# A second attention whose SP queue issues the next loads between the rows of maxima and the second shares, with the rows in one transfer

## The chip, the cores and the metric

The kernel runs on one core of a Trainium2 chip. Its engines are TensorE (PE in the profile; PEld is its weight load), VectorE (DVE), ScalarE (ACT), GpSimd (POOL) and SyncE (SP). SP computes nothing here: it waits on semaphores and issues DMA transfers, in the order in which they are written. The metric is the device time of one execution in microseconds (us), as the median of several runs.

## The reference, cut to what matters

Two transformer layers over 4 sequences of 1024 tokens with 256 columns. Each layer is attention and then a feed-forward part, with a layer norm behind each. The second layer's attention, which the change touches, has 8 heads of 32 columns:

```python
scores = jnp.einsum('bhqd,bhkd->bhqk', q, k) * scale
causal = jnp.tril(jnp.ones((T, T), dtype=bool))
scores = jnp.where(causal[None, None], scores, -jnp.inf)
...
attn = jax.nn.softmax(scores, axis=-1)
out = jnp.einsum('bhqk,bkhd->bqhd', attn, v).reshape(B, T, C)
return out @ w_out
```

The product with w_out, a residual sum, a layer norm and the routing of tokens to 16 experts follow on the same tokens, and then the experts themselves.

## The kernel before

The function phase_layer1 computes the second attention in 16 groups: 4 sequences (batches) times 4 pairs of heads. A group takes 12 rounds on PE, numbered i = 0 to 11. A round multiplies one tile of keys with a block of 512 queries for both heads (L2822, into PS), ACT takes the exponential (L2919), POOL masks the diagonal tiles (L2874), and some rounds later PE multiplies with the values (L2801, into PO).

**Maxima run ahead.** A softmax needs each query's maximum before its exponentials. PE therefore computes plain score products (L2774, into one of two tiles PM) for a group one or two ahead, twelve tiles for each group, and DVE reduces each tile (take, L2958). PE may write a tile of PM only when DVE has taken what stood in it. In the rounds 0 to 5 of group g these products belong to group g + 1, and from round 6 on to group g + 2: at round 6 PE waits for the queries and keys of group g + 2 (the semaphore q_in). In round 7 PE transposes the finished maxima of group g + 1 (L2785), ACT copies them to mrows (L2903), and SP sends them as two extra rows under the queries of that group (rows, L2711). They are needed at round 0 of group g + 1.

**Loads.** Queries, keys and values have 4 buffers. load(g) issues three transfers of queries, three of keys (256 KB each, L1558) and one of values (512 KB, L1569): 2 MB. SP issues load(g + 3) in group g.

**Sums and shares.** When a half (512 queries) of a group is done, ACT copies it out (L2911) and SP sends the row totals (L1785) and the unnormalised sums (L1790) to their places. DVE inverts the totals (L1917), SP stores them to DRAM (L1797, store_shares), waits for that, and reads them back spread over 32 partitions for each head (L1810, load_shares, 128 KB). Half 0 of group g - 1 is fetched at the start of SP's pass for group g, half 1 of group g - 1 behind the rows of group g + 1. When all four groups of a batch have their shares, DVE multiplies sums with shares (L1939, "weigh"): half 0 in round 7 and half 1 in round 11 of the first group of the next batch, that is of the groups 4, 8 and 12. These instructions stand in DVE's one queue between the reductions of L2958. PE then projects with w_out (L1849).

**Order.** There is no scheduler. Each engine's program is a Python loop, and an engine runs its instructions in the order in which that loop wrote them; SP's loop is the one in the function under block.sync.

The lines on which round 6 and the weighing wait are these:

```python
if t == 0 and ahead <= left:
    pe.wait_ge(q_in[(g + ahead) % BUFS], ((g + ahead) // BUFS + 1) * Q_TURNS)
...
dve.wait_ge(self.sums_in[i], self.SUM_DMAS * HG1 * (b + 1))
dve.wait_ge(self.shares_in[i], 16 * HG1 * (b + 1))
```

Of the kernel before, what the change touches and what calls it, by code (L numbers as in the profile page):

```python
# [6 lines left out]
F32 = mybir.dt.float32  # L7
# [11 lines left out]
TPB = SEQ // P  # L19
# [22 lines left out]
HALVES1 = 2  # L42
# [514 lines left out]
def phase_attention0(nc, d, keep, weights, stacks, shared):  # L557
# [25 lines left out]
    MROWS = R0 * PAIRS0 * HALVES1 * TPH  # L583
    ROW_DMAS = 16 * R0 * PAIRS0
    ONES_DMAS = 16 * BUFS * R0
# [31 lines left out]
    def head_of(g, s):  # L617


        return s % G0 if g == GROUPS - 1 and s // G0 > WIDE_FROM // G0 else ORDER[s % G0]  # L620
# [44 lines left out]
    with ExitStack() as ctx:  # L665
# [104 lines left out]
        def _(pool):  # L770
# [27 lines left out]
            for u in range(TURNS):  # L798
                cut_maxima(u)
                if u in FETCHES:  # L800

                    pool.wait_ge(rows_in, (u + 1) * ROW_DMAS)
                    weights.fetch(pool, d, FETCHES[u])
# [8 lines left out]
                if 0 <= first < ZERO_DMAS:  # L812
# [3 lines left out]
                    else:  # L816
                        pool.wait_ge(zero_out, 16 * first)
                    pool.wait_ge(rows_in, (u + 1) * ROW_DMAS)
                    for n in range(first, first + BLANKS):
# [14 lines left out]
        def _(pe):  # L834
# [44 lines left out]
            def score(g, s):  # L879
# [4 lines left out]
                if s % (UNITS // HALVES) == 0:  # L884
                    pe.wait_ge(rows_in, (HALVES * g + half + 1) * ROW_DMAS)
                p, r = head_of(g, s) // R0, head_of(g, s) % R0
# [58 lines left out]
        def _(act):  # L945
# [6 lines left out]
            def copy_rows(u):  # L952
                mine = slice(u % HALVES * MROWS, (u % HALVES + 1) * MROWS)
                act.wait_ge(m_turned, u + 1)
                if u >= HALVES:
                    act.wait_ge(rows_in, (u + 1 - HALVES) * ROW_DMAS)
                act.activation(mrows[mine], PT[mine], ACT.Copy).then_inc(m_copied, 1)
# [76 lines left out]
G1 = 2  # L1034
# [516 lines left out]
def load_keys1(sp, d, g, q, k, arrived):  # L1551


    hg, tok = g % HG1, slice(g // HG1 * SEQ, (g // HG1 + 1) * SEQ)
    for stack, side, first_blk in ((q, 0, 0), (k, 1, 2)):
        for s, pair in enumerate(PAIRS1):
            rows = d["qk1"][pair[side] * 4 + first_blk + hg // 2, (hg % 2) * 64:(hg % 2) * 64 + 64, tok]
            sp.dma_start(stack[s * D1:(s + 1) * D1].bitcast(F32), rows.rearrange("(j p) n -> p j n", p=D1)).then_inc(arrived, 16)  # L1558
# [8 lines left out]
def load_values1(sp, d, g, v, arrived):  # L1567
    src = values1(d, g // HG1)[g % HG1]
    sp.dma_start(v[:].rearrange("p t j c -> p (t j c)"), src.rearrange("p i c -> p (i c)")).then_inc(arrived, 16)  # L1569
# [1022 lines left out]
def phase_layer1(nc, d, keep, weights, tokens, shared):  # L2592


    K = len(PAIRS1) * D1
    KM = K + HALVES1
    BUFS = HG1
# [13 lines left out]
    GAP = SBANKS  # L2611
    TURN_PLACE = (TURN + 1) * G1
    LAPS = UNITS + GAP
    ROW_DMAS = 16 * HALVES1
    Q_TURNS = K1_TURNS
    LATE_TOTALS = (10, 6)
    assert STEPS % MTILES == 0 and LAPS % SBANKS == 0 and UNITS % RING == 0 and ROUNDS % PAIRED == 0
# [39 lines left out]
    with ExitStack() as ctx:  # L2657
# [3 lines left out]
        qst = [shared.q1] + [a.sb(f"qst{i}", [P, G1, SEQ], F32R) for i in range(1, BUFS)]  # L2661
# [7 lines left out]
        mrows = a.sb("mrows", [HALVES1 * G1 * TPB, P])  # L2669
# [12 lines left out]
        m_step, m_cut, m_turned, m_copied, rows_in = (  # L2682
            a.sem(n) for n in ("m_step", "m_cut", "m_turned", "m_copied", "rows_in"))
        scores, exped, masked, pv_done, out_copied = (
            a.sem(n) for n in ("scores", "exped", "masked", "pv_done", "out_copied"))
        route = Routing(nc, ctx, const, weights, tokens, shared, PM, max_taken, entry)
# [13 lines left out]
        @block.sync  # L2700
        def _(sp):
            def load(g):
                hg = g % BUFS
                load_keys1(sp, d, g, qst[hg], kst[hg], q_in[hg])
                load_values1(sp, d, g, vst[hg], v_in[hg])

            def rows(g):

                sp.wait_ge(m_copied, g + 1)
                for i in range(HALVES1):  # L2710
                    sp.dma_start(qst[g % BUFS][K + i:K + i + 1].bitcast(F32), mrows[i * G1 * TPB:(i + 1) * G1 * TPB, :])\  # L2711
                      .then_inc(rows_in, 16)

            def sums(g, half):
                sp.wait_ge(out_copied, g * HPS + half + 2)
                route.send_sums(sp, outT, g, half)

            sp.wait_ge(shared.ffn_stored, shared.FFN_DMAS)
            load(1)
            rows(0)  # L2720
            load(2)
            route.load_weights(sp, d)
            for g in range(GROUPS):
                if g > 0:
                    sums(g - 1, 1)
                    route.load_shares(sp, d, g - 1, 0)
                    route.store_shares(sp, d, g - 1, 1)
                sums(g, 0)
                if g + 1 < GROUPS:
                    rows(g + 1)  # L2730
                if g > 0:
                    route.load_shares(sp, d, g - 1, 1)
                if g + BUFS - 1 < GROUPS:
                    if g > 0:

                        sp.wait_ge(pv_done, g * ROUNDS + RING // G1)
                    load(g + BUFS - 1)
                if g == GROUPS - 3:
                    route.wait_sums_free(sp, BATCH - 2)
                    weights.load_up(sp, d, bass.ds(0, 1), 0)  # L2740
                if g == GROUPS - 2:
                    route.wait_shares_free(sp, BATCH - 2)
                    weights.load_down(sp, d, bass.ds(0, 1), 0)
                route.store_shares(sp, d, g, 0)
            route.load_shares(sp, d, GROUPS - 1, 0)
            sums(GROUPS - 1, 1)
            route.store_shares(sp, d, GROUPS - 1, 1)
            route.load_shares(sp, d, GROUPS - 1, 1)
            for n in range((BATCH - 1) * HPS, BLOCKS):
                sp.wait_ge(route.x3_done, (n + 1) * TPK)  # L2750
                tokens.store(sp, d, n, tokens.last_x3_out)
            route.wait_sums_free(sp, BATCH - 1)
            route.wait_shares_free(sp, BATCH - 1)
            weights.load_up(sp, d, bass.ds(1, 1), 1)
            weights.load_down(sp, d, bass.ds(1, 1), 1)
            sp.wait_ge(route.scattered, 16 * TOP_K * TILES)
            experts_sp(sp)

        @block.tensor
        def _(pe):  # L2760
# [45 lines left out]
            def slot(g, i):  # L2806
# [3 lines left out]
                if i == 0:  # L2810
                    pe.wait_ge(rows_in, (g + 1) * ROW_DMAS)
                ahead, t = 1 + (AHEAD + i) // STEPS, (AHEAD + i) % STEPS
# [183 lines left out]
def program(nc, d):  # L2996
    d["shares0"] = nc.dram_tensor("shares0", [H0, TOKENS], F32).ap()
    d["sums1"] = nc.dram_tensor("sums1", [SUM_ROWS, DIM], F32).ap()
    d["shares1"] = nc.dram_tensor("shares1", [H1, TOKENS], F32).ap()
    d["halves0"] = nc.dram_tensor("halves0", [HALVES1 * QK_BLK, P, TOKENS], F32).ap()  # L3000
    with ExitStack() as ctx:
        keep = {"const": ctx.enter_context(nc.sbuf_tensor("const", [P, C_COLS], F32))}
        shared = Shared(nc, ctx)
        with ExitStack() as layer0:
            weights = Layer0Weights(nc, layer0)
            with ExitStack() as attention:
                stacks = Stacks0(nc, attention, shared)
                phase_qkv0(nc, d, keep, stacks, shared)
                phase_attention0(nc, d, keep, weights, stacks, shared)
            phase_ffn0(nc, d, keep, weights, shared)  # L3010
        with ExitStack() as layer1:
            weights = ExpertWeights(nc, layer1, shared)
            tokens = Routed(nc, layer1, shared)
            phase_layer1(nc, d, keep, weights, tokens, shared)
# [54 lines left out]
```

## Time and profile before

| | |
|---|---|
| median of 3 runs | 1913.09 us (1911.92 to 1913.39) |
| profiled execution | 1909.37 us, its span 1907.4 us |
| second attention in the span | about 1143 to 1536 us |
| PE busy share of the span | 94% |
| DVE, ACT, POOL busy share | 75%, 59%, 28% |

Times in rows are counted from the span's start. What an engine waited for stands in brackets behind the row of the instruction that waited. "SPq" rows are instructions that issue transfers; their duration is that of the issue, not of the transfer. A granted TensorE clock of 1.00 is 2.4 GHz, 0.50 is 1.2 GHz.

### The profile page before, as it was taken

The numbers are of one execution on the slowest core, as the hardware profiler recorded it, in microseconds if no ns is written. First come the engines' busy times: TensorE is split into PE (matmuls) and PEld (weight loads), VectorE is DVE, ScalarE is ACT, GpSimd is POOL, SyncE is SP. The second block draws the span as 40 slices with busy tenths as digits, with TensorE's granted clock in tenths as the row PEclk, the third lists the DMA queues.
The fourth block names the chain that finished last, engine by engine and source line by source line (L and its number), as shares of the span: only waits on it lengthen the run. The fifth ranks groups of instructions, "written<-read, shape, count | busy, mean of one in ns | idle before, by whom it ended". The sixth has DMA issues, their size and how long they took to land. (4 is left out here: it accounts for less than half of the span.)

```text
span 1907.4 us, 34604 instructions
## 1 busy us (share of the span) xinstructions
PE 1795.9 (94%) x12690; PEld 1170.9 (61%) x12690; DVE 1429.7 (75%) x2814; ACT 1117.3 (59%) x2212; POOL 528.6 (28%) x686
## 2 busy tenths in 40 slices
PE   8989999999999999799999989999999987999994
PEld 4545444444444444388888865555555566999994
DVE  7879999999999999367677655466666554766665
ACT  4645888888888888622333214446463632655555
POOL 5760000233000001032223212212525243444444
PEclk9986999999999999899999988999999998999997
DMA  4883744565434502023444255546666334655555
GB/s 170 280 260 53 124 79 96 131 144 122 86 57 73 83 28 85 20 76 111 153 143 147 89 188 120 137 100 156 153 154 156 97 107 147 150 144 144 145 115 196
DMA packets 146600, 239.18 MB, mean 125 GB/s; under 512 B 25830, under 2 KB 81159, under 8 KB 146449
## 3 DMA queue, kind: packets, MB, share of 16 engines
q1 hardware_dynamic: 113312, 171.48, 36.8%
q0 software_dynamic: 17024, 34.25, 7.0%
q10 hardware_dynamic: 16112, 31.46, 4.5%
q8 instruction: 92, 1.51, 0.3%
q14 instruction: 60, 0.48, 0.1%
HBM read 137.49 MB, written 96.60 MB: 123 GB/s over the span
## 5 line engine op out<-in xcount | busy, mean ns | idle before, releaser
L994 DVE TENSOR_REDUCE b_mx<-b_PM 128x1 f32<-128x512 f32 x1024 | 621.0, 679 | 17.9 <-PE b_PM L848 17.5
L970 ACT ACTIVATE b_probs<-b_PS 128x512 f32<-128x512 f32 x1000 | 523.9, 606 | 69.1 <-PE b_PS L902 53.8
L848 PE MATMUL b_PM<-b_kst,b_qst 48*128 48x512 f32 x888 | 280.9, 430 | 0.0
L2919 ACT ACTIVATE d_probs<-d_PS 128x512 f32<-128x512 f32 (+3 forms) x384 | 166.5, 496 | 183.2 <-PE d_PS L2822 182.5
L902 PE MATMUL b_PS<-b_qst,b_kst 50*128 50x512 f32 x744 | 256.9, 436 | 2.1 <-issue 0.2
L2958 DVE TENSOR_REDUCE d_mx<-d_PM 128x2 f32<-128x1024 f32 (+1 forms) x192 | 179.9, 950 | 101.5 <-PE d_PM L2774 59.3
L902 PEld LDWEIGHTS b_PS<-b_qst,b_kst 50*128 50x128 f32 x744 | 120.4, 184 | 163.4 <-ACT b_probs L970 147.4
L2874 POOL TENSOR_SCALAR_AFFINE_SELECT d_probs<-d_probs 128x128 f32<-128x128 f32 x256 | 74.6, 305 | 268.1 <-ACT d_probs L2919 263.4
L790 POOL CAST b_mhalves<-b_maxima 128x16 fp32r<-128x16 f32 x32 | 6.3, 197 | 505.3 <-DVE b_maxima L1003 505.3
L848 PEld LDWEIGHTS b_PM<-b_kst,b_qst 48*128 48x128 f32 x888 | 142.0, 184 | 5.4
L874 PE MATMUL b_PO<-b_probs,x_v 128*32 128x384 f32 (+2 forms) x2048 | 145.2, 390 | 0.0
L874 PE MATMUL b_PO<-b_probs,b_vst 128*32 128x384 f32 (+3 forms) x1960 | 143.0, 397 | 1.0 <-ACT b_probs L970 0.9
L1257 POOL TENSOR_TENSOR c_hT<-c_hidden,c_hT 128x512 fp32r<-128x512 f32 x48 | 64.8, 1350 | 218.1 <-DVE c_hT L1504 218.1
L2562 DVE TENSOR_TENSOR f_h_low<-f_h,f_h_high 128x512 fp32r<-128x512 f32 x96 | 66.5, 692 | 72.8 <-ACT f_h_high L2352 72.8
L2822 PE MATMUL d_PS<-d_qst,d_kst 98*128 98x512 f32 (+3 forms) x288 | 106.3, 386 | 8.6 <-ACT d_probs L2919 4.1
L2385 POOL DMA_INDIRECT sums<-f_y,f_to x44 | 88.8, 2019 | 90.2 <-ACT f_y L2333 72.2
L848 PE MATMUL b_PM<-x_k,x_q 48*128 48x512 f32 x291 | 108.0, 508 | 3.0 <-DVEq L986 2.7
L2774 PE MATMUL d_PM<-d_kst,d_qst 96*128 96x512 f32 (+3 forms) x288 | 102.0, 372 | 3.0 <-DVE d_mx L2958 3.0
L902 PE MATMUL b_PS<-x_q,x_k 50*128 50x512 f32 x256 | 91.5, 448 | 0.6
L2822 PEld LDWEIGHTS d_PS<-d_qst,d_kst 98*128 98x128 f32 x288 | 53.9, 191 | 49.9 <-issue 32.5
L1276 PE MATMUL c_PG<-c_x1T,u_w_gate 128*128 128x512 f32 x288 | 76.7, 402 | 5.5 <-DVE c_hidden L1502 4.1
L2333 ACT ACTIVATE f_y<-f_y,f_coef 128x256 f32<-128x256 f32 x44 | 22.4, 510 | 95.2 <-DVE f_y L2540 95.2
(318 smaller groups left out, 3753.9 us busy)
## 6 DMA issues: line engine op xcount, KB each, us to landing
halves<-a_parts SPq DMA_DIRECT2D x7, 2048.0 KB, 8.7
qk<-c_halves ACTq DMA_DIRECT2D x7, 2048.0 KB
w_w<-L_ffn_fc1T SPq DMA_DIRECT2D x12, 1024.0 KB, 5.0
w_w<-L_ffn_fc2T SPq DMA_DIRECT2D x12, 1024.0 KB, 6.3
b_qst<-halves SPq DMA_DIRECT2D x72, 128.0 KB, 4.4
b_kst<-halves SPq DMA_DIRECT2D x72, 128.0 KB, 7.6
d_qst<-qk SPq DMA_DIRECT2D x36, 256.0 KB, 5.2
d_kst<-qk SPq DMA_DIRECT2D x36, 256.0 KB, 7.4
```

The costliest lines, as they stand in the source:

```text
L848: mm = pe.matmul(PM[n % MBANKS][:], qst[buf][at, p, first:first + P], kst[buf][at, p, kh * BLK:(kh + 1) * BLK], start=True, stop=True)
L874: mm = pe.matmul(PO[j * VS0:(j + 1) * VS0, cols], vst[g % BUFS][:, kt, j, :], probs[:, (R * G0 + i) % RING, cols], start=(kt == 0 and firs ...
L902: pe.matmul(score_bank(g, s)[:], kst[g % BUFS][at, p, kt * P:(kt + 1) * P], qst[g % BUFS][at, p, half * BLK:(half + 1) * BLK], start=True, ...
L970: act.activation(probs[:, s % RING], score_bank(g, s)[:], ACT.Exp).then_inc(exped, 1)
L994: dve.tensor_reduce(mx[:, half, (r * PAIRS0 + p) * TPH + t, kh:kh + 1], PM[n % MBANKS][:], AX.X, ALU.max)\
L1276: mm = pe.matmul(out, lhs(left, c), rhs(right, c), start=(k == 0 and c == 0), stop=(k == len(PAIRS1) - 1 and c == chunks - 1))
L2385: pool.indirect_dma_start(out=d["sums1"], out_offset=bass.IndirectOffsetOnAxis(ap=index.bitcast(U32), axis=0), in_=src, in_offset=None, bo ...
L2774: mm = pe.matmul(PM[n % MTILES][:, j, 0:w], qst[g % BUFS][0:K, j, qt * P:(qt + 1) * P], kst[g % BUFS][0:K, j, kh * BLK:kh * BLK + w], star ...
L2822: pe.matmul(PS[bank(s)][:, 0:w], kst[g % BUFS][0:KM, j, kt * P:(kt + 1) * P], qst[g % BUFS][0:KM, j, q0:q0 + w], start=True, stop=True).th ...
L2874: pool.affine_select(out=near, in_=near, pattern=[[1, P]], compare_op=ALU.is_ge, fill=0.0, base=0, channel_multiplier=-1)\
L2919: act.activation(probs[:, s % RING, 0:w], PS[bank(s)][:, 0:w], ACT.Exp).then_inc(exped, 1)
L2958: dve.tensor_reduce(mx[:, :, qt, kh], PM[n][:, :, 0:keys(qt, kh)], AX.X, ALU.max).then_inc(max_taken[n], 1)
```

## The change

In each group's pass of SP's loop, the load of group g + 3, with its wait on pv_done, now stands directly behind the rows of maxima, and load_shares for half 1 of group g - 1 behind the load; before it was the other way round. The two row transfers (one for the high halves, one for the low halves) become one transfer with two destination partitions, and the count that the readers wait for is halved to match.

```diff
-    ROW_DMAS = 16 * HALVES1
+    ROW_DMAS = 16
...
                 sp.wait_ge(m_copied, g + 1)
-                for i in range(HALVES1):
-                    sp.dma_start(qst[g % BUFS][K + i:K + i + 1].bitcast(F32), mrows[i * G1 * TPB:(i + 1) * G1 * TPB, :])\
-                      .then_inc(rows_in, 16)
+                sp.dma_start(qst[g % BUFS][K:KM].rearrange("i j n -> i (j n)").bitcast(F32), mrows[:]).then_inc(rows_in, 16)
...
                 if g + 1 < GROUPS:
                     rows(g + 1)
+                if g + BUFS - 1 < GROUPS:
+                    if g > 0:
+
+                        sp.wait_ge(pv_done, g * ROUNDS + RING // G1)
+                    load(g + BUFS - 1)
                 if g > 0:
                     route.load_shares(sp, d, g - 1, 1)
-                if g + BUFS - 1 < GROUPS:
-                    if g > 0:
-
-                        sp.wait_ge(pv_done, g * ROUNDS + RING // G1)
-                    load(g + BUFS - 1)
```

SP's queue in the pass for group 4, before. x_q1_60 and its like are the query and key buffers of the first group of four, d_qst1 to d_qst3 those of the others; w_w2 holds the shares and w_w1 the sums:

```order
L1790 DMA w_w1<-d_outT 32x512 x2
L2711 DMA d_qst1<-d_mrows 1x16x128 x2
L1810 DMA w_w2<-shares1 64x1x512
L1558 DMA d_qst3<-qk1 32x2x1024 x3
L1558 DMA d_kst3<-qk1 32x2x1024 x3
L1569 DMA d_vst3<-v1 128x1024
L1797 DMA shares1<-e_totals 2x64x8
```

The same place now:

```order
L2710 DMA d_qst1<-d_mrows 2x16x128
L1558 DMA d_qst3<-qk1 32x2x1024 x3
L1558 DMA d_kst3<-qk1 32x2x1024 x3
L1569 DMA d_vst3<-v1 128x1024
L1810 DMA w_w2<-shares1 64x1x512
L1797 DMA shares1<-e_totals 2x64x8
```

The seven transfers of a load have moved ahead of the one that fetches shares, and two row transfers are one. The passes for the groups 1 to 12 change in this way; those for 13 to 15 have no load, and in the pass for group 0 there are no shares to fetch.

DVE's queue in rounds 6 to 12 of the same group 4, where the shares are used (L2958 is a reduction of maxima, L1939 the weighing, L1952 the residual sum of the projected block, L1946 statistics for the norm):

```order
L2958 TENSOR_REDUCE d_mx<-d_PM 128x2 x2
L1917 RECIPROCAL e_totals<-e_totals 128x8
L1952 TENSOR_TENSOR e_x<-e_x,d_PM 128x1024
L2958 TENSOR_REDUCE d_mx<-d_PM 128x2
L1939 TENSOR_TENSOR w_w<-w_w 128x512
L1946 BN_STATS e_stats<-e_x 128x6 x2
L2958 TENSOR_REDUCE d_mx<-d_PM 128x2
L1939 TENSOR_TENSOR w_w<-w_w 128x512
L1946 BN_STATS e_stats<-e_x 128x6 x2
L2958 TENSOR_REDUCE d_mx<-d_PM 128x2 x2
```

Nothing moved here: the changed kernel has the same rows with line numbers that are lower by two for the lines of phase_layer1.

## Rows read from the trace of the kernel before

**Rows 1.** The page: the span, and the chain that ended last by engine.
```profile
span 1907.4 us, 34604 instructions
...
PE 28%; DVE 4%; DMA 4%; ACT 2%; issue 2%; SPq 1%; POOL 1%; POOLq 0%; DVEq 0%; ACTq 0%
```

**Rows 2.** Waits, 1140 to 1535 us: engine, line, releaser; total us, times, longest.
```profile
PE d_PS L2822 <- DMA d_kst<-qk: 6.4, 3, 2.8
```

**Rows 3.** Timeline of PE, round 6 of groups 2, 3, 8, 12: start, duration, instruction, wait.
```profile
1204.15 0.50 PE L2822 MATMUL d_PS<-d_qst,d_kst 98*128 98x512 f32 x1 [1.74 <-DMA x_k<-qk]
...
1227.26 0.50 PE L2822 MATMUL d_PS<-d_qst,d_kst 98*128 98x512 f32 x1 [2.76 <-DMA d_kst<-qk]
...
1349.18 0.50 PE L2822 MATMUL d_PS<-x_q,x_k 98*128 98x512 f32 x1 [1.66 <-DMA d_kst<-qk]
...
1450.45 0.50 PE L2822 MATMUL d_PS<-x_q,x_k 98*128 98x512 f32 x1 [1.97 <-DMA d_kst<-qk]
```

**Rows 4.** Timeline of SP, pass of group 4.
```profile
1255.15 1.22 SPq L2711 DMA_DIRECT2D d_qst<-d_mrows  x2
1256.41 0.57 SPq L1810 DMA_DIRECT2D w_w<-shares  x1
1257.03 1.37 SPq L1558 DMA_DIRECT2D d_qst<-qk  x3
...
1259.85 0.43 SPq L1569 DMA_DIRECT2D d_vst<-v  x1
1261.00 0.56 SPq L1797 DMA_DIRECT2D shares<-e_totals  x1
```

**Rows 5.** Timelines of SP and of DVE: a fetch of shares with quiet queues.
```profile
1250.37 0.56 SPq L1810 DMA_DIRECT2D w_w<-shares  x1
...
1255.17 0.69 DVE L1939 TENSOR_TENSOR w_w<-w_w 128x512 f32<-128x512 f32 x1 [2.22 <-DMA w_w<-shares]
```

**Rows 6.** Windows: stretch, us; PE, PEld, DVE, ACT, POOL busy; PEclk, DMA share, GB/s.
```profile
1254.00:1255.00 1.00, 1.00 (x6) 0.37 (x3) 0.00 (x0) 0.00 (x0) 0.00 (x0) 1.00 0.17 25
1258.00:1268.00 10.00, 10.00 (x57) 6.91 (x54) 6.38 (x10) 3.10 (x8) 2.38 (x8) 1.00 0.99 215
```

**Rows 7.** Timeline of SP, pass of group 2: a store behind a load, and its waiter.
```profile
1217.71 0.56 SPq L1797 DMA_DIRECT2D shares<-e_totals  x1
...
1229.13 0.56 SPq L1810 DMA_DIRECT2D w_w<-shares  x1
```

**Rows 8.** The chain in order of time: the same store with quiet queues.
```profile
1533.64 4.67 DMA shares<-e_totals
```

**Rows 9.** DMA issues of groups 4, 8, 12: the values; the last number is us to landing.
```profile
d_vst<-v SPq DMA_DIRECT2D x1, 512.0 KB, 10.4
...
d_vst<-v SPq DMA_DIRECT2D x1, 512.0 KB, 11.6
...
d_vst<-v SPq DMA_DIRECT2D x1, 512.0 KB, 10.9
```

**Rows 10.** Timeline of DVE, round 11 of group 4: half 1 is weighed.
```profile
1264.63 0.68 DVE L1939 TENSOR_TENSOR w_w<-w_w 128x512 f32<-128x512 f32 x1
```

**Rows 11.** Timeline of PE, group 5, round 2: the product, then the projection.
```profile
1268.04 0.40 PE L2774 MATMUL d_PM<-d_kst,d_qst 96*128 96x512 f32 x1
...
1269.62 3.69 PE L1849 MATMUL d_PM<-e_wout,w_w 128*128 128x256 f32 x16 [0.83 <-DVE d_mx L2958]
```

**Rows 12.** Windows with the granted clock (PEclk), columns as in Rows 6.
```profile
1204.00:1208.00 4.00, 3.61 (x21) 2.02 (x21) 0.43 (x1) 2.66 (x6) 0.00 (x0) 1.00 0.21 65
1228.00:1234.00 6.00, 6.00 (x19) 2.45 (x18) 1.32 (x3) 2.76 (x6) 0.00 (x0) 0.50 0.16 41
1351.00:1354.00 3.00, 3.00 (x11) 1.13 (x11) 0.76 (x2) 1.38 (x4) 1.02 (x2) 0.51 0.31 110
1453.00:1456.00 3.00, 3.00 (x8) 0.64 (x8) 0.76 (x2) 0.65 (x3) 0.29 (x1) 0.50 0.23 76
1545.00:1548.00 3.00, 2.95 (x7) 2.41 (x8) 2.97 (x3) 0.00 (x0) 2.39 (x3) 0.52 0.21 66
```

**Rows 13.** Timeline of PE behind the last group: what came before the last window.
```profile
1545.05 5.41 PE L1849 MATMUL d_PM<-e_wout,w_w 128*128 128x256 f32 x16 [2.00 <-DVE w_w L1939]
```

More of the change, by code:

```diff
@@ L2730, in _ @@
                     rows(g + 1)
-                if g > 0:
-                    route.load_shares(sp, d, g - 1, 1)
                 if g + BUFS - 1 < GROUPS:
@@ L2737, in _ @@
                     load(g + BUFS - 1)
+                if g > 0:
+                    route.load_shares(sp, d, g - 1, 1)
                 if g == GROUPS - 3:
```

## The prediction

> **What bounds the kernel now.** I start from the page. The chain that ended last runs mostly through PE [rows 1], so a change on SP's queue counts only where PE ends up waiting for a transfer. The waits of the second attention name such a place: PE, before L2822, waited for keys three times [rows 2], and PE's timeline shows a fourth, listed under x_k [rows 3]. All four are at round 6 of a group, where PE turns to maxima of the group two ahead: 1.74, 2.76, 1.66 and 1.97 us, together **8.13 us**. The other groups' loads land before round 6.
>
> A wait costs more than itself. After the wait of 2.76 us the granted clock was 0.50 for 6 us, after those of 1.66 and 1.97 us it was 0.51 and 0.50 for 3 us each, and after that of 1.74 us it stayed at 1.00 [rows 12]. PE was busy throughout these stretches, so half speed cost 3.0 + 1.5 + 1.5 = **6.0 us**. So 14.1 us hang on loads that arrive late.
>
> Next, SP's timeline in a pass that loads: rows of maxima at 1255.15, the fetch of half 1's shares at 1256.41, the load from 1257.03 to 1260.28 [rows 4]. Between the first row transfer and the load lie 1.88 us. And the fetch of shares is a slow transfer: with quiet queues it was issued at 1250.37 and DVE could use it at 1255.17, after 4.80 us for 128 KB, and the DMA share meanwhile was 0.17, which is some 2.7 engines of 16 [rows 5, 6]. A load has a share of 0.99 [rows 6]. So the fetch runs on two or three engines and, standing ahead of the load, makes these the last to finish it.
>
> **What the change removes.** (1) One row transfer, half of 1.22 us of issue, and the issue of the fetch, 0.57 us, with its gap, no longer stand ahead of the load. The load starts 1.88 - 0.65 = 1.23 us earlier behind the rows [rows 4]. (2) The engines that carried the fetch begin the load at once. This is worth between nothing and 4.80 - 0.56 = 4.24 us [rows 5]; since part of that is latency, I take 2.5. (3) Against this, the merged row transfer has two destination partitions instead of one each. No row of before shows it. The store of shares has two rows too, of 64 pieces each, and took 4.67 us on quiet queues [rows 8]; the rows of maxima have 16 pieces each. Bounds are 0 and 4.67 us; a quarter would be 1.2, and with the fixed part taken off I take 0.7 us. It stands ahead of the load. The rows themselves are needed only at the next group's round 0, four rounds on, and even 4.67 us of flight stays inside that.
>
> The sum of (1) to (3) is 1.23 + 2.5 - 0.7 = 3.0 us, more than the longest of the four waits. I count **7.6 us** of the 8.13 as gone (0.5 for a wait that survives in part, since in group 2 DVE also waits for totals queued behind a load), and the 6.0 us of clock with them: **-13.6 us**. If (2) is worth nothing, the load gains 0.5 us, four waits shrink by 2.1 us together, and the clock may stay as it is.
>
> The Trainium skill, "DMA: Bandwidth & Descriptors", section "Why a DMA increments its semaphore by 16 and not by 1", says that a copy uses the largest number of engines up to 16 that divides the slowest dimension of both sides. By that rule the fetch (two heads outermost) and the merged rows (two partitions outermost) would each run on two engines, and the two old row transfers on 16 each. The share of 0.17 agrees for the fetch; no row of before shows it for the merged rows.
>
> **What the change adds.** The fetch of half 1 now stands behind 2 MB. Who waits for it? In most groups nobody: DVE weighs once in a batch. But in the groups 4, 8 and 12 it weighs half 1 in round 11, three rounds after the pass's rows. In group 4 DVE started this at 1264.63 without any wait [rows 10]; there are three such places, and in the other two the distance from the issue of the values is the same within 0.2 us. Before, the fetch issued at 1256.41 landed near 1256.41 + 4.80 = 1261.2, so the cover was 3.4 us.
>
> A transfer behind a load is late. The small store issued at 1217.71, right behind a load, released its waiter at 1229.13, after 11.4 us instead of 4.67 [rows 7, 8]. The values, last of the load, landed 10.4, 11.6 and 10.9 us after their issue in the groups 4, 8 and 12 [rows 9]. The engines that carry the fetch did the same work then as they will do now, with the fetch first instead of last. So I take the landing of the values before as the landing of the fetch after, moved up because this work starts at 1255.15 and not at 1256.41 (1.26 us), and back by 0.7 us for the merged rows: 0.56 us earlier. Group 4: 1259.85 + 10.4 - 0.56 = 1269.7, against 1264.63: 5.1 us late. The issue of the values is 4.78 us ahead of the weighing, so for 8 and 12: 11.6 - 4.78 - 0.56 = 6.3 and 10.9 - 4.78 - 0.56 = 5.6. DVE stands still for **17.0 us** in three places.
>
> Who stands behind it? DVE's queue is in order: behind the weighing stand the reductions of L2958, which free the tiles of PM. PE can go on for two rounds, until its product at 1268.04, 3.4 us after the weighing began; then it needs the reduction that follows statistics of 0.7 us and takes 1.2 us. The projection behind waits for DVE already now, 0.83 us at 1269.62 [rows 11], so DVE sets the pace there and nothing absorbs the delay, save the 0.3 to 0.4 us that DVE itself idles between: 17.0 - 3 x 0.3 = **+16.1 us** on PE. And PE then idles some 5 us at a stretch. Behind an idle of 2.00 us the clock was 0.52 for 3 us [rows 12, 13], behind 2.76 us it was 0.50 for 6: 1.5 to 3.0 us lost each time, 2.2 in the middle, three times: **+6.6 us**.
>
> The store of the next totals (L1797) is also pushed back on SP by nothing: it waited until 1261.00 for DVE, and load and fetch are issued by 1259.7.
>
> The sum: +16.1 + 6.6 - 13.6 = **+9.1 us**. The profiled execution took 1909.37 us, so it would be 1918.5; it ran 3.7 us below the median of the three runs. On the median: 1913.09 + 9.1 = **1922.2 us**.
>
> **The rivals.** A: the shares come in time. If a small transfer on few engines is not held up by the load, the fetch, issued at about 1259.1, lands 4.80 us later, at 1263.9, before 1264.63. The point from which it decides is 5.5 us of flight. Then only the gain is left: 1913.1 - 13.6 = 1899.5 us, faster. For it speaks that the load is spread over all engines and may leave gaps; against it the store that took 11.4 us. The Trainium skill, same page, section "Queues, rings and completion order", says that each engine consumes a ring in order; by that rule the fetch can't overtake, and the trace's store agrees.
>
> B: the shares are late as computed, but the clock holds in the new waits, as it did after 1.74 us (the fetch in group 8 or 12 may also be earlier by 0.6 us than group 4's shift says): +16.1 - 13.6 = +2.5, or with a shorter delay about 0: 1914.4 us, no change that shows.
>
> C: the cost comes, the gain doesn't: the four waits shrink by 2.1 us only, since the load itself, at a DMA share of 0.99, sets the landing, and the clock falls as before. +16.1 + 6.6 - 2.1 = +20.6: 1933.7 us. Against it: a load needs its 10 us either way, but starts earlier. A milder form (waits gone, clock not) gives +15.1: 1928.2 us.
>
> That the change doesn't do what it says is excluded for SP: its queue has the new order.
>
> **How the numbers follow.** Forecast 0.56, its own range 1915 to 1930; A 0.17; B 0.15; C with its milder form 0.12. The predicted time is the forecast's. The range of 1908 to 1931 leaves out A and the full form of C (0.03): it takes in B. A measurement of this kernel can tell 0.2% (3.8 us) from no change. Faster by more: A and 0.03 of B, 0.20. Within: 0.12 of B and 0.08 from the forecast's lower end, 0.20. Slower: 0.60.
>
> **What would show it.** In the changed kernel's profile: at round 6 of the groups 2, 3, 8 and 12 no wait of PE for d_kst or x_k, or one under 0.5 us, and a clock of 1.00 behind it. L1939's second place in groups 4, 8 and 12 waits 5 to 6 us for w_w<-shares; PE then waits 4 to 6 us for DVE before L2774, and the clock falls to 0.50 for 3 to 6 us. The values land after 8 to 9 us instead of 10.4 to 11.6. I am wrong if L1939 doesn't wait (A), or if the waits at round 6 keep more than half their length (C).

## The result, and the profile after

| | before | after |
|---|---|---|
| median | 1916.85 us of 18 runs | 1928.1 us of 18 runs |
| lowest and highest | 1911.45 to 1925.43 | 1922.09 to 1935.82 |
| ratio | | 1.0066 (95%: 1.0051 to 1.0081) |
| profiled execution | 1909.37 us, span 1907.4 | 1923.44 us, span 1921.7 |
| granted TensorE clock, mean of the span | 0.961 | 0.958 |

The changed kernel is slower by 0.0066 x 1916.85 = 12.6 us; the forecast was +9.1 us. Its page has these lines for [rows 1]:

```profile
span 1921.7 us, 34588 instructions
...
PE 28%; DVE 4%; issue 3%; DMA 2%; ACT 2%; SPq 2%; POOL 0%; POOLq 0%; DVEq 0%; ACTq 0%
```

**The gain's side.** The waits between 1140 and 1550 us (engine, line, releaser; total us, times, longest) have no row of PE waiting for keys any more, the row that stood in [rows 2]. PE's round 6 in groups 2, 3, 8 and 12 starts without a wait of the kind shown in [rows 3]. The two rows that matter now are these:

```profile
DVE w_w L1939 <- DMA w_w<-shares: 22.2, 6, 6.2
PE d_PM L2772 <- DVE d_mx L2956: 14.8, 16, 5.2
```

Of the 22.2 us, 14.3 stand where half 1 is weighed in the groups 4, 8 and 12; of the 14.8 us, 11.4 stand right behind these three places. The rest of the first row stands where half 0 is weighed, and DVE waited there in the kernel before too.

**The cost's side.** SP's timeline for group 4 (start, duration of the issue, instruction) answers to [rows 4]. One row transfer of 0.67 us stands where two took 1.22, the load follows at 1248.51, and the fetch is issued behind it, at 1253.65:

```profile
1247.79 0.67 SPq L2710 DMA_DIRECT2D d_qst<-d_mrows  x1
1248.51 1.34 SPq L1558 DMA_DIRECT2D d_qst<-qk  x3
...
1253.18 0.43 SPq L1569 DMA_DIRECT2D d_vst<-v  x1
1253.65 0.56 SPq L1810 DMA_DIRECT2D w_w<-shares  x1
```

The chain that ended last, in order of time, now runs through this fetch and through DVE, where in round 11 of group 4 there had been no wait [rows 10]:

```profile
1253.65 8.24 DMA w_w<-shares
...
1261.98 0.69 DVE w_w L1939
1262.67 0.66 DVE e_stats L1946 x2
1263.34 1.12 DVE d_mx L2956
```

The timelines of DVE and of PE show the same place in the groups 4, 8 and 12. First DVE, where half 1 is weighed (the wait stands in brackets):

```profile
1261.98 0.69 DVE L1939 TENSOR_TENSOR w_w<-w_w 128x512 f32<-128x512 f32 x1 [4.65 <-DMA w_w<-shares]
...
1369.09 0.69 DVE L1939 TENSOR_TENSOR w_w<-w_w 128x512 f32<-128x512 f32 x1 [6.22 <-DMA w_w<-shares]
...
1475.57 0.69 DVE L1939 TENSOR_TENSOR w_w<-w_w 128x512 f32<-128x512 f32 x1 [3.40 <-DMA w_w<-shares]
```

Then PE, two and a half microseconds later each time, waiting for a tile of PM that DVE has not yet reduced; the group 4 place answers to [rows 11]:

```profile
1264.52 0.71 PE L2772 MATMUL d_PM<-d_kst,d_qst 96*128 96x512 f32 x1 [3.70 <-DVE d_mx L2956]
...
1371.63 0.80 PE L2772 MATMUL d_PM<-d_kst,d_qst 96*128 96x512 f32 x1 [5.25 <-DVE d_mx L2956]
...
1478.10 0.50 PE L2772 MATMUL d_PM<-d_kst,d_qst 96*128 96x512 f32 x1 [2.44 <-DVE d_mx L2956]
```

A reader should see the order: a transfer is late, an engine waits that is not the bottleneck, and because that engine's queue is in order, the bottleneck waits for something that has nothing to do with the transfer.

Windows around these places (stretch; busy of PE, PEld, DVE, ACT, POOL; granted clock, DMA share, GB/s) answer to [rows 12]. The clock falls behind the new waits, the first, second and fourth row. It also falls in group 12 ahead of the weighing, the third row, with PE busy throughout. Around round 6 of groups 2, 3 and 8, the last three rows, it is 1.00:

```profile
1264.00:1272.00 8.00, 6.88 (x17) 5.24 (x18) 3.45 (x6) 0.38 (x1) 0.29 (x1) 0.57 0.11 33
1370.00:1378.00 8.00, 5.87 (x15) 4.49 (x16) 4.56 (x8) 0.38 (x1) 1.29 (x2) 0.57 0.14 44
...
1466.00:1470.00 4.00, 4.00 (x13) 3.17 (x12) 0.21 (x2) 0.00 (x0) 0.14 (x1) 0.57 1.03 256
...
1479.00:1484.00 5.00, 3.91 (x11) 3.28 (x12) 2.07 (x4) 0.14 (x1) 1.29 (x2) 0.66 0.23 72
1204.00:1210.00 6.00, 5.76 (x31) 2.72 (x31) 2.81 (x4) 3.39 (x8) 1.16 (x4) 1.00 0.26 59
1224.00:1233.00 9.00, 8.78 (x48) 4.43 (x48) 4.24 (x6) 4.83 (x13) 2.24 (x8) 1.00 0.43 106
1349.00:1355.00 6.00, 5.14 (x25) 2.31 (x27) 1.65 (x4) 2.93 (x7) 3.05 (x5) 1.00 0.50 136
```

**The two sides in the two traces.** Take the start of round 7, where PE transposes the maxima, in each group, and subtract before from after. The difference is -5.4 us in group 3 and -7.4 in group 4, -0.7 in group 5, +4.8 in group 9, +2.8 in group 12 and +9.9 in group 14. It falls at the old waits of round 6 and rises at the three weighings. By these steps the early loads brought about 7.4 + 1.7 + 2.0 = 11.1 us and the weighings cost 6.6 + 7.3 + 7.2 = 21.1 us, clock included, in this pair of executions. The two spans differ by 14.3 us; the remaining 4.4 us come behind group 14, where no load moved, and this pair can't tell whose they are.

### The profile page after: what moved, and what is told of

Its sections match the earlier page's. It is cut to its first block and busy times, and to the rows that moved or that the text cites. A ratio compares the mean times of both kernels' runs of the same rounds, so it can differ in the third digit from the quotient of the medians.

```text
span 1921.7 us, 34588 instructions
## 1 busy us (share of the span) xinstructions
PE 1804.2 (94%) x12690; PEld 1177.1 (61%) x12690; DVE 1430.4 (74%) x2814; ACT 1117.2 (58%) x2212; POOL 528.0 (27%) x686
## 5 line engine op out<-in xcount | busy, mean ns | idle before, releaser
L2772 PE MATMUL d_PM<-d_kst,d_qst 96*128 96x512 f32 (+3 forms) x288 | 102.6, 373 | 14.8 <-DVE d_mx L2956 14.8
L1276 PE MATMUL c_PG<-c_x1T,u_w_gate 128*128 128x512 f32 x288 | 76.6, 402 | 5.5 <-DVE c_hidden L1502 4.1
```

The lines of the kernel that those rows point to most:

```text
L2772: mm = pe.matmul(PM[n % MTILES][:, j, 0:w], qst[g % BUFS][0:K, j, qt * P:(qt + 1) * P], kst[g % BUFS][0:K, j, kh * BLK:kh * BLK + w], star ...
```

## Experiments

Theory: the three late fetches at the groups 4, 8 and 12 are the whole cost, and the early loads elsewhere are a gain. Rivals: the merged row transfer costs or gains by itself; the early loads bring little. Each experiment is compared with runs of the kernel before made beside it. Intervals are 95%.

### One row transfer alone

The kernel before, with the two row transfers merged and nothing moved.

```diff
-    ROW_DMAS = 16 * HALVES1
+    ROW_DMAS = 16
...
-                for i in range(HALVES1):
-                    sp.dma_start(qst[g % BUFS][K + i:K + i + 1].bitcast(F32), mrows[i * G1 * TPB:(i + 1) * G1 * TPB, :])\
-                      .then_inc(rows_in, 16)
+                sp.dma_start(qst[g % BUFS][K:KM].rearrange("i j n -> i (j n)").bitcast(F32), mrows[:]).then_inc(rows_in, 16)
```

> The kernel before with the merged row transfer alone; the fetch of shares stays ahead of the load. Theory L (late shares cost some 21 us at the three weighings, early loads give back some 11): the load starts 0.5 us earlier, the waits at round 6 shrink by at most 0.5 us each, so 0 to -3 us. Rival R (the merged rows, on few engines, delay what stands behind them): +3 us or more, and the waits at round 6 grow.

Measured: 0.9991 (0.9973 to 1.0009), medians 1913.53 and 1914.51 us. In the time, the merged transfer costs and gains nothing that can be told. In its trace PE's waits for keys, [rows 2], come to 3.1 us in three places instead of 8.13 in four, a larger fall than the expected 0.5 us each. That is one execution; in the time no gain shows, though the interval leaves room for 5 us.

### The new order alone

The kernel before with the load ahead of the fetch in every group and two row transfers.

```diff
                     rows(g + 1)
+                if g + BUFS - 1 < GROUPS:
+                    if g > 0:
+                        sp.wait_ge(pv_done, g * ROUNDS + RING // G1)
+                    load(g + BUFS - 1)
                 if g > 0:
                     route.load_shares(sp, d, g - 1, 1)
-                if g + BUFS - 1 < GROUPS:
...
```

> The kernel before with the load moved ahead of the fetch in all groups, rows still as two transfers. Theory L: nearly the whole change, +8 to +13 us, DVE waits 4 to 6 us at each of the three weighings of half 1. Rival R: most of the loss was the merged rows, so this is within 3 us of the kernel before, or faster.

Measured: 1.0076 (1.0050 to 1.0102), median 1928.72 us: +14.6 us (9.6 to 19.5), a little over the expected 8 to 13, and the same as the full change within the intervals. DVE's weighing in group 4 waited 5.03 us for the shares and PE 4.06 us behind it. The order makes the whole difference.

### The order at all groups but 4, 8 and 12

The changed kernel, with the old order in the three groups that weigh.

```diff
+                def load_ahead():
...
+                weighed = g % HG1 == 0
+                if not weighed:
+                    load_ahead()
                 if g > 0:
                     route.load_shares(sp, d, g - 1, 1)
+                if not (not weighed):
+                    load_ahead()
```

> The changed kernel, but in the groups 4, 8 and 12 (where half 1 is weighed) the fetch stands ahead of the load again. Theory L: only the gain is left, no wait of DVE for shares at half 1's weighing, no wait of PE at round 6: -8 to -14 us against the kernel before. Rival C (the waits at round 6 and the clock behind them don't go): 0 to -3 us.

Measured: 0.9971 (0.9951 to 0.9991), median 1909.67 us. The cost is gone, and so are the waits of round 6: the trace has none, nor a wait at the weighings. But the gain is 5.6 us (1.7 to 9.4) and not 8 to 14. Its trace shows a place where clock went: in three stretches of 14 us each (the third from 1510 to 1524, clock 0.53) PE was busy throughout, no wait of note ran ahead of them, and the clock was half. Before the first of them the clock was 1.00, as the first row has it:

```profile
1285.00:1290.00 5.00, 4.74 (x32) 2.94 (x28) 3.19 (x9) 4.80 (x12) 1.19 (x5) 1.00 1.04 231
1298.00:1312.00 14.00, 13.80 (x52) 8.71 (x52) 4.09 (x13) 4.23 (x8) 0.00 (x0) 0.51 0.16 43
1403.00:1417.00 14.00, 13.80 (x52) 8.63 (x52) 4.11 (x13) 4.23 (x8) 0.00 (x0) 0.53 0.25 68
```

The profile of the kernel before has no such stretch in its second attention. But this execution took 1919.41 us, 9.7 above its kernel's median, and lost more to the clock than any other of the twelve, so three stretches are not its usual number. What the kernel keeps of the gain is better read from the means over all runs, in the table further down.

### The order at the groups 4, 8 and 12 alone

The kernel before with `if weighed: load_ahead()` ahead of the fetch, and behind it for the other groups.

> The kernel before with the load ahead of the fetch only in the groups 4, 8 and 12. Theory L: only the cost, +18 to +24 us: PE idles 4 to 6 us three times and runs at half clock behind each. If the clock holds, +14 to +17. Rival R: +/-2 us.

Measured: 1.0132 (1.0102 to 1.0161), median 1938.43 us: +25 us (19 to 31), nearly twice the full change. PE's timeline has both sets of waits, those of round 6 (the first two rows) and those behind the weighing (the third, and likewise 4.51 and 4.81 us in the groups 8 and 12):

```profile
1206.29 0.50 PE L2829 MATMUL d_PS<-d_qst,d_kst 98*128 98x512 f32 x1 [1.94 <-DMA x_k<-qk]
...
1229.29 0.69 PE L2829 MATMUL d_PS<-d_qst,d_kst 98*128 98x512 f32 x1 [2.63 <-DMA d_kst<-qk]
...
1274.78 0.79 PE L2781 MATMUL d_PM<-d_kst,d_qst 96*128 96x512 f32 x1 [4.53 <-DVE d_mx L2965]
```

So the change is the sum of two parts of opposite sign, and they can be had apart: +25 and -5.6 make +20, more than the +12.6 of both together. The intervals of the three (6 us either side for this one, 4 for the one above) just allow a difference of this size. A part of it may be real: the three waits of PE are 13.9 us together here and 11.4 in the changed kernel, and the table further down puts the whole excess on the clock.

### Weighing later

If DVE's wait is the cost, half 1 can be weighed two rounds later, in round 13 instead of 11, in the changed kernel.

```diff
-    WEIGH, WEIGH_LAST = (7, 11), (1,)
+    WEIGH, WEIGH_LAST = (7, 13), (1,)
```

> The changed kernel with half 1 weighed in round 1 of the next group instead of round 11, two rounds (some 4 us) later on DVE and still ahead of its projection. Theory L: DVE waits 0 to 2 us instead of 3.4 to 6.2 us, PE waits no more than 1.5 us, and the gain of the early loads comes out: -3 to -8 us against the kernel before, where the changed kernel is 12.6 us slower. Rival Q (what costs is the load and the fetch on the DMA engines, whoever waits): it stays at +8 us or more.

Measured: 1.0055 (1.0033 to 1.0077), median 1922.23 us against 1913.95. The expectation of -3 to -8 us fell: this is no repair. DVE's wait did shrink, to 0.35, 1.56 and 2.16 us. But the projection reads what DVE weighs, and PE now waits there, for the product itself and not for a tile of PM:

```profile
1266.80 5.19 PE L1849 MATMUL d_PM<-e_wout,w_w 128*128 128x256 f32 x16 [2.92 <-DVE w_w L1939]
...
1372.15 5.41 PE L1849 MATMUL d_PM<-e_wout,w_w 128*128 128x256 f32 x16 [4.17 <-DVE w_w L1939]
...
1477.45 5.68 PE L1849 MATMUL d_PM<-e_wout,w_w 128*128 128x256 f32 x16 [4.77 <-DVE w_w L1939]
```

Take DVE's wait from PE's and the rest is the same each time: 2.92 - 0.35, 4.17 - 1.56 and 4.77 - 2.16 are all 2.6 us. PE would wait that long even for shares in time, since the weighing, in two steps with a reduction between them, now ends right ahead of the projection. So two thirds of PE's 11.9 us were put there by the experiment's own edit. It neither confirms nor refutes that DVE's wait is the cost; the two experiments above do that.

### The fetch on a queue of its own

The changed kernel, but in groups 4, 8 and 12 ACT issues the fetch, in round 9, so that it stands behind nothing in SP's queue.

```diff
-                if g > 0:
+                if g % HG1 > 0:
                     route.load_shares(sp, d, g - 1, 1)
...
+                    if i == TURN + 2 and g > 0 and g % HG1 == 0:
+                        route.load_shares(act, d, g - 1, 1)
```

> The changed kernel, but in the groups 4, 8 and 12 ACT issues the fetch of half 1's shares in round 9, on its own queue, after SP issued the load. Theory F (the fetch was late because it stood behind 2 MB in SP's queue): the fetch lands within 5 to 7 us of its issue, DVE waits 0 to 3 us instead of 3.4 to 6.2 us, total 0 to +6 us against the kernel before. Rival G (the DMA engines are full during a load, whatever the queue): DVE still waits 3 us or more each time, +9 us or more.

Measured: 1.0050 (1.0032 to 1.0069), median 1924.97 us against 1915.85. In group 4 ACT began to issue it at 1248.19, SP began the load at 1248.33, and DVE still waited for the shares until 1261.14: 13.0 us of flight. (ACT's issue lasted 1.11 us, so it isn't shown which of the two reached the DMA engines first.) The rows are one of ACT's timeline, one of SP's and one of DVE's:

```profile
1248.19 1.11 ACTq L1810 DMA_DIRECT2D w_w<-shares  x1
...
1248.33 1.35 SPq L1558 DMA_DIRECT2D d_qst<-qk  x3
...
1261.14 0.69 DVE L1939 TENSOR_TENSOR w_w<-w_w 128x512 f32<-128x512 f32 x1 [3.94 <-DMA w_w<-shares]
```

In the other two groups it was issued at 1361.77 and 1469.08 and used after 13.8 and 14.4 us, behind waits of 6.54 and 6.08. Counted from the start of the load, the shares came after 12.8, 16.2 and 16.2 us, where in the changed kernel it was 13.5, 16.0 and 15.0. So it isn't SP's queue alone that holds the fetch up. The load in flight does: from ACT's queue the fetch came 0.7 us sooner in one group and no sooner in the other two. The Trainium skill, "DMA: Bandwidth & Descriptors", section "Issuing engines are not separate DMA queues", says that transfers from all issuing engines end up on the same DMA engines and interleave; this run agrees, as the fetch from ACT took 13.0 us beside the load.

### The fetch as two transfers, one per head

If the fetch is slow because it runs on two or three DMA engines, one transfer for each head, with the 32 partitions outermost, should be fast. It was tried on the kernel before and on the changed one.

```diff
-        share = d["shares1"][heads, tok].unsqueeze(1).to_broadcast([G1, D1, BLK])
-        to = hg * G1 * D1
-        sp.dma_start(self.shares[b % 2][to % P:to % P + G1 * D1, half, to // P], share).then_inc(self.shares_in[half], 16)
+        for j in range(G1):
+            head = hg * G1 + j
+            to = head * D1
+            share = d["shares1"][head:head + 1, tok].to_broadcast([D1, BLK])
+            sp.dma_start(self.shares[b % 2][to % P:to % P + D1, half, to // P], share).then_inc(self.shares_in[half], 16)
...
-                    dve.wait_ge(self.shares_in[i], 16 * HG1 * (b + 1))
+                    dve.wait_ge(self.shares_in[i], 16 * G1 * HG1 * (b + 1))
```

On the kernel before:

> The kernel before with the fetch by head alone, order and row transfers as before. Theory T: no engine is behind the others when the load starts, the four waits at round 6 shrink by 1.5 us or more each, a fetch with quiet queues lands in under 4 us instead of 4.8: -2 to -8 us. Rival U: one more issue of 0.6 us ahead of the load, the waits grow: 0 to +3 us.

Measured: 0.9964 (0.9949 to 0.9979), medians 1906.91 and 1913.95 us: 7.0 us faster. None of PE's waits at round 6 is left, though no load is issued earlier. And with quiet queues the fetch issued at 1241.56 on SP was used by DVE at 1244.67 without a wait, in 3.1 us or less instead of the 4.80 of [rows 5]. In group 8 DVE did wait, for a fetch issued at 1346.47, until 1349.76: 3.3 us. The DMA share rose to 0.61 from 1243.0 to 1243.5, where it was 0.17 in [rows 6]:

```profile
1241.56 0.80 SPq L1812 DMA_DIRECT2D w_w<-shares  x2
...
1244.67 0.68 DVE L1941 TENSOR_TENSOR w_w<-w_w 128x512 f32<-128x512 f32 x1
```

On the changed kernel:

> The changed kernel with the fetch of shares as two transfers, one for each head, so that the slowest dimension is 32 partitions on both sides and not 2 heads. Theory T (the fetch runs on two engines and so adds a tail of some 2.5 us behind the load): DVE's three waits shrink by 2 to 3 us each, +2 to +7 us against the kernel before. Rival U (the number of engines is not what makes the fetch slow): the waits stay, +11 to +15 us.

Measured: 1.0032 (1.0008 to 1.0056), median 1919.39 us. PE's waits behind the weighing shrink from 3.70, 5.25 and 2.44 us to 2.85, 2.10 and 0.99, and DVE's from 4.65, 6.22 and 3.40 to 3.80, 3.07 and 1.96. Counted from the start of the load, the shares came after 12.7, 13.0 and 11.9 us instead of 13.5, 16.0 and 15.0. So the fetch's own slowness accounted for 0.8 to 3.1 us of the delay, and the larger part is the 2 MB ahead.

Both at once, that is the changed order except in the groups 4, 8 and 12, one row transfer, and the fetch by head:

> The changed kernel with the fetch ahead of the load in the groups 4, 8 and 12 and by head everywhere. If early loads and the fetch by head remove the same waits at round 6, it equals the version without the fetch by head: -4 to -8 us against the kernel before. If the fetch by head also shortens the chain of totals and shares at the end of the attention: 2 to 3 us more.

Measured: 0.9965 (0.9949 to 0.9980), median 1907.75 us. Once the fetch is quick, the early load gives nothing more that can be told.

### The store by head as well

The small store of totals has two rows outermost too, so it was split in the same way, on top of the fetch by head in the kernel before.

```diff
...
-        sp.dma_start(d["shares1"][heads, tok].rearrange("h (c n) -> h c n", n=self.CUTS), self.totals[:, half])\
-          .then_inc(self.shares_out[half], 16)
+        for j in range(G1):
+            rows = slice(j * P // G1, (j + 1) * P // G1)
+            sp.dma_start(d["shares1"][hg * G1 + j, tok].rearrange("(c n) -> c n", n=self.CUTS), self.totals[rows, half])\
+              .then_inc(self.shares_out[half], 16)
...
```

> The kernel before with both the fetch and the store of shares as two transfers, one for each head; order and row transfers as before. Theory T (transfers with two heads outermost run on two engines): a store with quiet queues lands in under 3.5 us instead of 4.67, the chain behind the last group is shorter by 2 to 4 us than with the fetch by head alone: -7 to -12 us against the kernel before. If the extra issues eat this: -4 to -7 us.

Measured: 0.9960 (0.9943 to 0.9976), median 1908.47 us against 1915.85, the same as without it. The expected 2 us for each store were never there to win, and the timeline of SP in the kernel before tells why. The 4.67 us of [rows 8] are those of a store issued 0.6 us behind a fetch. A store with no fetch ahead of it, at 1545.14, let SP go on at 1547.42, after 2.28 us:

```profile
1533.03 0.56 SPq L1810 DMA_DIRECT2D w_w<-shares  x1
1533.64 0.56 SPq L1797 DMA_DIRECT2D shares<-e_totals  x1
1538.33 0.52 SPq L1810 DMA_DIRECT2D w_w<-shares  x1
1545.14 0.56 SPq L1797 DMA_DIRECT2D shares<-e_totals  x1
1547.42 0.56 SPq L1810 DMA_DIRECT2D w_w<-shares  x1
```

I had called the first of these a store on quiet queues. It was not: it stood behind the slow fetch. The kernel with the fetch by head alone bears this out. Its store issued at 1526.13, 1.3 us behind a quick fetch, let SP go on at 1528.42, after 2.29 us.

The same with the early loads of the third experiment and one row transfer added:

> The same with the merged rows and with the load ahead of the fetch except in the groups 4, 8 and 12. No wait at round 6 is left to remove, so the order gives nothing more: within 2 us of the kernel with fetch and store by head alone.

Measured: 0.9963 (0.9950 to 0.9977), median 1908.70 us. The four kernels with a fetch by head and no late fetch can't be told apart in time; the first of them is the simplest, and beats the kernel before by 7 us.

## Why the prediction was right, and where it was off

The sign, the mechanism and the places were right. That the size came out near, +9.1 against +12.6 us (9.8 to 15.5), was partly luck: both delays of PE were forecast too large and the net loss to the clock far too small (+0.6 against +9.4 us), and these errors made up for each other.

**The fetch is late at three places: right, a little too large.** Forecast were waits of 5.1, 6.3 and 5.6 us in DVE, 17.0 together. They were 4.65, 6.22 and 3.40, or 14.3. The method, landing of the values before as the landing of the fetch after, held within 0.5 us in the groups 4 and 8 and missed group 12 by 2.2. There it was not the fetch that came sooner. It landed 15.7 us after the rows were issued, just as forecast (1461.94 + 10.9 - 0.56 - 1456.57 = 15.7). But DVE was ready for it only 12.3 us after the rows, where before it had been 10.0, behind a projection of PE that took 5.38 us and not 3.69, at a clock of 0.57 from 1466 to 1470. The forecast had held DVE's own time fixed. Rival A, a fetch in time, fell: 8.3, 12.7 and 11.5 us lay between issue and use, where it needed less than 5.5.

**DVE's delay reaches PE: right.** The waits before L2772 are 3.70, 5.25 and 2.44 us, one within and two below the forecast of 4 to 6; a further 0.60, 0.51 and 1.13 us stand before the projection at L1849, where the kernel before waited 0.83 each time.

**The cost with the clock: 22.7 us forecast, 25 (19 to 31) measured** where it stood alone, and 21.1 by the steps between the two traces. The clock fell behind all three waits, so rival B fell with it. The sum held, its two terms did not, as the table shows: +16.1 us of delay were 8.5, and +6.6 us of clock were 16.7.

**The gain of the loads: the term of the sum that was mis-sized.** Forecast was -13.6 us, made of 7.6 us of waits and 6.0 us of clock. The waits went, all four. But the gain alone measured -5.6 us (1.7 to 9.4). Take span times granted clock as the time at full speed, and the remainder as the time lost to the clock; this supposes that PE sets the pace throughout. The means over the runs are these (the errors are one standard error of the mean; three sets of runs of the kernel before lie within 1.1 and 2.0 us of each other):

| kernel | at full speed, us | lost to the clock, us |
|---|---|---|
| before | 1835.0 +- 0.4 | 77.9 +- 0.8 |
| early loads, not at the weighings | 1829.8 +- 0.7 | 77.9 +- 1.9 |
| late fetches at the weighings only | 1843.5 +- 0.8 | 94.6 +- 1.0 |
| after (its own runs) | 1840.0 +- 0.3 | 87.3 +- 1.1 |
| before, fetch by head (its own before: 1835.7 +- 0.4 and 76.6 +- 0.7) | 1827.3 +- 0.4 | 77.6 +- 1.0 |

The early loads were worth 5.2 us at full speed (+- 0.8), not 7.6, and the 6.0 us of clock didn't come back: the loss is 77.9 us with and without the waits of round 6, give or take 2.1. The fetch by head, which removes the same waits, brought no clock back either, but 8.4 us at full speed; so why the early loads brought less than the 8.13 us of waits is open. The late fetches, by contrast, add 8.5 us of waiting and 16.7 us of clock, so there the clock was the larger part and the forecast had it as the smaller. At full speed the two parts add up to the change (8.5 - 5.2 = 3.3 us against 5.0 +- 0.5, each side with an error of about 1); in the loss they do not (16.7 + 0.0 against 9.4). I had taken from one execution that a half-speed stretch behind a wait is due to that wait. For those of round 6 the runs don't bear this out: behind the places where the waits had been the clock stayed at 1.00, but over the whole span as much was lost as before, in the one trace above in the three long stretches. "C, the cost comes, the gain doesn't" was right in its milder form (waits gone, clock not), which gave +15.1; the measured +12.6 lies between it and the forecast.

**The pieces of the load's gain.** That the slow fetch held up the loads is confirmed in a way the change itself can't show: with the fetch by head and no other edit the waits of round 6 are gone. The 0.7 us for the merged rows rested on the store's 4.67 us, which was not that of quiet queues, and the experiment with that edit alone shows no cost. The landing of the values, 8 to 9 us forecast, stands in no row of the changed kernel's three groups, so it isn't settled there. The values of six other groups, x_v in both traces, landed after 8.1 us in the changed kernel and 11.6 in the one before (medians), which agrees with the forecast.

The Trainium skill, "DMA: Bandwidth & Descriptors", section "Why a DMA increments its semaphore by 16 and not by 1", has a copy use as many engines, up to 16, as divide the slowest dimension of both sides. For the fetch, the runs agree: with 32 instead of 2 outermost it took 3.1 to 3.3 us instead of 4.8, though the edit also made two transfers of one, and no run separates the two. For the merged rows no run here shows a cost.

**Still open:** what makes the clock fall for 13 us in the rounds that route tokens, in executions that have no long wait ahead of it; and why the late fetches alone lose 7 us more to the clock than the whole change does.

## What to carry to other kernels

Before a transfer is moved behind a large load, look for the place where its data is used soonest, not where it is used on average: nine harmless places brought 5.6 us and three others took 25. If a small transfer is in a load's way, first ask why it is slow; splitting it so that the partitions stand outermost gave 7 us and moved nothing. And don't book the clock loss behind a wait as the wait's own until a run without the wait has shown it.

## What was unexpected of the hardware

A small transfer is slow beside a load even from another issuing engine, and even when its issue begins with the load's: 13.0 us from ACT's queue in that run, against 4.8 with quiet queues. Issued on SP behind the load it took 8.3 us, but that count begins 5.1 us later in the load; from the load's start the two were 12.8 and 13.5 us.

The granted clock makes more of the scatter between executions than the work does: of the kernel before, 25 executions beside the fetch by head lay within 9 us of each other in time at full speed and within 14 us in the loss to the clock; of the kernel with early loads not at the weighings, 12 lay within 7 and within 22 us. In the second attention of eight of the eleven experiments' profiles, eleven times in all, the clock fell to half for some 13 us while PE was busy throughout. Each time it fell at the same place of a group that routes tokens, where PE had just waited 0.2 us for DVE ahead of a product into PM. One is shown, in the kernel before with the fetch by head; the longest wait of PE in the 7 us ahead was 0.25 us:

```profile
1295.00:1309.00 14.00, 13.88 (x51) 8.70 (x52) 4.01 (x13) 4.20 (x8) 0.00 (x0) 0.51 0.16 41
```
